# Queries times attention in a linear-attention kernel: from four products of 128 rows to eight of 64 rows at two row positions

## The reference

```
xn = layernorm(x);  q, k, v = xn @ Wq + bq, xn @ Wk + bk, xn @ Wv + bv
q = softmax(q, over the features of a head);  k = softmax(k, over the tokens)
attn[e, d] = sum over tokens s of k[s, e] * v[s, d]          # one small square per head
y[t, :]    = q[t, :] @ attn                                  # the "mix", per head
h = silu(layernorm(y) * (1 + scale) + shift) @ Wo + bo;  x = x + h
```

## Time and profile before

| | |
|---|---|
| median of 3 runs | 888.93 us (888.59 to 888.94) |
| the profiled execution | 892.45 us |
| its span in the trace | 890.7 us |
| TensorE busy (matmuls) | 847.7 us, 95% |
| VectorE, ScalarE, GpSimd busy | 683.3, 607.1, 550.8 us |
| mean granted clock of TensorE | 0.987 |

### The profile page before, as it was taken

How to read it: one execution, slowest core, us unless ns; L and a number is a source line. 1 busy time by engine, 2 the same in 40 slices (tenths; PEclk the granted TensorE clock), 3 DMA queues, 4 the chain that set the end, 5 groups by cost and what they waited for, 6 DMA issues and landing times.

```text
span 890.7 us, 19760 instructions
## 1 busy us (share of the span) xinstructions
PE 847.7 (95%) x6581; PEld 717.9 (81%) x6581; DVE 683.3 (77%) x1356; ACT 607.1 (68%) x1441; POOL 550.8 (62%) x741
## 2 busy tenths in 40 slices
PE   4988999899999999999987999999999999999997
PEld 4876878788787888888866878888888888888885
DVE  6976777687786787788876877877877788777665
ACT  6366676676666767777776767767766777776664
POOL 2566765666656657666756766676667666765641
PEclk9998999999999999999999999999999999999999
DMA  8686665666666555555664655566666556656431
GB/s 295 239 275 204 195 213 191 201 198 208 178 198 215 174 195 172 185 177 171 196 185 166 216 165 181 179 199 185 193 194 198 188 186 189 195 178 201 155 132 60
DMA packets 115482, 169.79 MB, mean 191 GB/s; under 512 B 11806, under 2 KB 84630, under 8 KB 115382
## 3 DMA queue, kind: packets, MB, share of 16 engines
q1 hardware_dynamic: 114880, 168.08, 59.4%
q10 hardware_dynamic: 502, 0.46, 0.2%
HBM read 95.61 MB, written 72.88 MB: 189 GB/s over the span
## 4 chain that ended last, share of the span: by engine, by line
PE 69%; DMA 11%; DVE 7%; ACT 4%; issue 4%; SPq 4%; POOL 1%; ACTq 0%; DVEq 0%; POOLq 0%
PE PS L943 60%; PE PS L1037 5%; DMA qy_turned<-QS 4%; PE PS L1021 3%; SPq L402 2%; DMA QT<-qy_turned 2%; DMA k_turned<-KT 1%; DMA x_turned<-XS 1%; SPq L417 1%; DMA STAGE<-in_wq 1%; DMA EK<-k_turned 1%; DMA XT<-x_turned 1%; ACT XF L786 1%; ACT SK L696 1%; SPq L377 1%
## 5 line engine op out<-in xcount | busy, mean ns | idle before, releaser
L592 POOL TENSOR_TENSOR HL<-H,HH 128x512 fp32r<-128x512 f32 x60 | 78.2, 1303 | 196.4 <-ACT HH L767 192.9
L734 ACT ACTIVATE Z<-QT,FC,FA 128x128 f32<-128x128 f32 x240 | 99.4, 486 | 114.4 <-DMA QT<-qy_turned 114.4
L943 PE MATMUL PS<-XH,WH_k 128*128 128x256 f32 x512 | 150.9, 295 | 3.9 <-DVE WL_k L319 3.9
L943 PE MATMUL PS<-XL,WH_k 128*128 128x256 f32 x512 | 145.7, 285 | 0.0
L943 PE MATMUL PS<-XH,WL_k 128*128 128x256 f32 x512 | 145.6, 284 | 0.0
L943 PE MATMUL PS<-WH_o,HH 128*128 128x512 f32 x248 | 106.8, 431 | 15.1 <-issue 14.8
L804 ACT ACTIVATE XN<-X,NBX,RSX 128x512 f32<-128x512 f32 x60 | 48.9, 815 | 82.4 <-POOL NBX L541 82.4
L943 PEld LDWEIGHTS PS<-XH,WH_k 128*128 128x128 f32 x512 | 99.0, 193 | 4.4 <-issue 4.2
L696 ACT ACTIVATE SK<-SK,KN 128x128 f32<-128x128 f32 x256 | 99.1, 390 | 3.5 <-DVE KN L1243 3.5
L943 PE MATMUL PS<-WH_q,XH 128*128 128x512 f32 x256 | 101.4, 396 | 0.0
L943 PE MATMUL PS<-WL_o,HH 128*128 128x512 f32 x248 | 101.0, 407 | 0.0
(11 more groups left out here) (155 smaller groups left out, 2121.5 us busy)
## 6 DMA issues: line engine op xcount, KB each, us to landing
qy_turned<-QS SPq DMA_DIRECT2D x60, 512.0 KB, 2.9
QT<-qy_turned SPq DMA_DIRECT2D x240, 128.0 KB, 3.0
k_turned<-KT SPq DMA_DIRECT2D x32, 512.0 KB, 4.1
EK<-k_turned SPq DMA_DIRECT2D x128, 128.0 KB, 2.8
x_turned<-XS SPq DMA_DIRECT2D x30, 512.0 KB, 2.9
XT<-x_turned SPq DMA_DIRECT2D x120, 128.0 KB, 3.4
out_x<-X SPq DMA_DIRECT2D x32, 256.0 KB, 3.4
X<-in_x SPq DMA_DIRECT2D x9, 512.0 KB, 5.3
```

The source lines that it names most:

```text
L592: eng.tensor_tensor(hl_of(o), h_of(o), hh_of(o).bitcast(F32), ALU.subtract).then_inc(pool_hl, 1)
L734: z = eng.activation(z_of(o)[:, c * P:c * P + P].rearrange("p (q n) -> p q n", q=Q), src, ACT.Identity, bias=FC[l][:, c, b:b + 1], scale=F ...
L943: mm = eng.matmul(dst, left[a](c), right[b](c), start=(c == 0 and a + b == 0), stop=(c == C - 1 and a == 1))
```

## The change

The contraction of the mix is cut in two. For each chunk c and each half u, 64 rows of EQ are the weights, at row position 0 or 64 of the array, and 66 columns stream through: for two heads of 32 (or one head of 64 as two pieces of 32), one column for the sum and 32 columns of the head. Half u writes to bank B_Y + u. That is eight products of 64x66 in place of four of 128x132. ATT shrinks from 128x528 to 128x264 elements, the attention products write into 256 columns of their bank instead of 512, the ScalarE copy reads 256 columns and writes them in runs of 32 with one column left free between them, and VectorE reads y in the new order (pieces of 33, the first the sum). The order of the work on every engine is as before; there are ten fewer rows of memsets on VectorE.

```
--- before.py
+++ after.py
-        ATT = sb("ATT", [P, 2, 2 * (P + Q)])
+        ATT = sb("ATT", [P, C, 2 * (32 + 1)])
...
-                eng.activation(ATT[:, :, Q:Q + 2 * P], PS[:, B_ATT, :].rearrange("p (b n) -> p b n", b=2), ACT.Copy)\
-                   .then_inc(act_att, 1)
+                eng.activation(ATT[:, :, :].rearrange("p c (h n) -> p (c h) n", h=2)[:, :, 1:],
+                               PS[:, B_ATT, 0:2 * P].rearrange("p (k n) -> p k n", n=32), ACT.Copy).then_inc(act_att, 1)
...
                 for c in range(C):
                     for f in range(0, P, 32):
                         a = f // w * w
+                        to = 64 * c + a % 64
                         vs = v[:, c * P + a:c * P + a + w]
                         ks = EK[:, f // 32, c // 2, t, c % 2, :]
-                        mm = eng.matmul(PS[f:f + 32, B_ATT, c * P + a:c * P + a + w],
+                        mm = eng.matmul(PS[f:f + 32, B_ATT, to:to + w],
                                         vs if l == 0 else ks, ks if l == 0 else vs,
                                         start=True, stop=True, tile_position=(0, f))
...
-                W = P + Q
+                W = 2 * (32 + 1)
                 for c in range(C):
-                    mm = eng.matmul(bank(B_Y + c // 2, (c % 2) * W, W), EQ[:, c * P:c * P + P],
-                                    ATT[:, c // 2, (c % 2) * W:(c % 2 + 1) * W], start=True, stop=True)
+                    for u in range(2):
+                        r = slice(64 * u, 64 * u + 64)
+                        mm = eng.matmul(bank(B_Y + u, c * W, W), EQ[r, c * P:c * P + P], ATT[r, c, :],
+                                        start=True, stop=True, tile_position=(64 * u, 0))
                 mm.then_inc(pe_y, 1)
...
-                ps = PS[:, B_Y:B_Y + 2, 0:Q]
-                sums = bass.AP(tensor=ps.tensor, offset=ps.offset, ap=[ps.ap[0], ps.ap[1], [Q + 2 * P, 2], [1, Q]])
-                then(eng.reciprocal(RQ[:, :].rearrange("p (b s q) -> p b s q", b=2, s=2), sums))
+                got = PS[:, B_Y:B_Y + 2, 0:2 * C * 33].rearrange("p u (k n) -> p u k n", n=33)
+                sums = RQ[:, :].rearrange("p (u k n) -> p u k n", u=2, n=1)
+                then(eng.reciprocal(sums, got[:, :, :, 0:1]))
...
-                eng.tensor_tensor(y.rearrange("p (b h n) -> p b h n", b=2, n=32),
-                                  PS[:, B_Y:B_Y + 2, Q:Q + 2 * P].rearrange("p b (h n) -> p b h n", n=32),
-                                  RQ[:, :].rearrange("p (b h) -> p b h", b=2).unsqueeze(3).to_broadcast([P, 2, 8, 32]),
+                five = [P, 2, C, 2, 32]
+                eng.tensor_tensor(y.rearrange("p (c u h n) -> p u c h n", c=C, u=2, h=2),
+                                  got[:, :, :, 1:33].rearrange("p u (c h) n -> p u c h n", h=2),
+                                  sums.rearrange("p u (c h) n -> p u c h n", h=2).to_broadcast(five),
                                   ALU.mult).then_inc(dve_yr, 1)
```

More of the change, by code:

```diff
@@ L1284, in second_ones @@
             def second_ones():
-                w = HEAD[1]
                 eng.wait_ge(pe_y, B)
[L1288 to L1291, removed]
+                for h in range(2):
+                    ins = eng.memset(ATT[:, :, 33 * h:33 * h + 1], 1.0)
                 ins.then_inc(dve_ones, 1)
@@ L1296, in zero_attention @@
                 eng.wait_ge(act_xf, 2 * FIRST)
-                eng.memset(PS[:, B_ATT, :], 0.0).then_inc(dve_zero, 1)
+                eng.memset(PS[:, B_ATT, 0:2 * P], 0.0).then_inc(dve_zero, 1)
             def mixed(j):
                 eng.wait_ge(pe_y, j + 1)
-                ps = PS[:, B_Y:B_Y + 2, 0:Q]
-                sums = bass.AP(tensor=ps.tensor, offset=ps.offset, ap=[ps.ap[0], ps.ap[1], [Q + 2 * P, 2], [1, Q]])
-                then(eng.reciprocal(RQ[:, :].rearrange("p (b s q) -> p b s q", b=2, s=2), sums))
+                got = PS[:, B_Y:B_Y + 2, 0:2 * C * 33].rearrange("p u (k n) -> p u k n", n=33)
+                sums = RQ[:, :].rearrange("p (u k n) -> p u k n", u=2, n=1)
+                then(eng.reciprocal(sums, got[:, :, :, 0:1]))
                 eng.wait_ge(dve_ys, min(j, LAST_Y))
@@ L1368, in start @@
                     a, z = 32 * g, 32 * g + 32
-                    eng.memset(ATT[a:z, :, g:g + 1], 1.0)
-                    eng.memset(ATT[a:z, :, 2 * P + Q + g:2 * P + Q + g + 1], 1.0)
+                    eng.memset(ATT[a:z, :, 33 * (g % 2):33 * (g % 2) + 1], 1.0)
                 eng.tensor_reduce(FOLD[:, :], ident[:, :].rearrange("p (g b) -> p b g", b=B), AX.X, ALU.add)
```

## The result

The kernel became slower: 900.74 us (897.34 to 905.36) against 888.93, ratio 1.0134, interval 1.0086 to 1.0181. The forecast was 904.4 us, with 880 to 916 as its range. The profiled execution took 905.36 us with a span of 903.6, so 12.9 us more than that of before. Times are medians, a ratio is worked out from the single executions and so is not exactly that of the medians. The ratios leave out executions over 1.5% above the fastest of their kernel, here two of the twelve of `eighths` (902.20 and 902.32 us).

A forecast was written before the change was run, and what follows sets the result against it. TensorE, busy 95% of the span, was taken to bound the kernel; 20.5 us for 64 longer mixes, less 0.2 for the copy and 4.8 for waits, gave +15.5 on 888.93: 904.4 us, range 880 to 916.

The forecast's parts named there:

- the sum: One mix, last output matmul to second keys matmul: 1.57 us against 1.25; 64 mixes give +20.5 us.
- the fold's rows: Conditioning fold: 128x128 float32 loads with 32 streamed columns also start 0.112 us apart, so the load sets the pace.
- Rival 2: Mix: the positions halve the work; -8 us (881), or -29 us (860) without entry and exit costs; chance 0.13.
- column positions: Attention: four column positions load side by side, 0.054 us for each four; two row positions assumed alike, eight pairs at 0.112.
- Rival 1: Mix: the two row positions load one after another, 16 at 0.112 us; +73 us, 962; chance 0.17.
- The turns: Going into and out of the divided array at each mix drains the engine; +0.32 us a mix.
- Entry: From the last output matmul to the mix's first matmul: 0.32 us, where an undivided one comes after 0.23.
- the load in the open: The mix's first weight load, no longer hidden: 0.10 us.
- exit: From the mix's last matmul to the recorded keys product: 0.15 us, where it was 0.04.
- the signs to look for: New trace: 1.5 to 1.6 us around a mix, first keys matmul 0.15 after it, 0.30 to the second.
- rival 3: Mix: nothing changes, since half rows need no change of array mode; 887 to 892 us; chance 0.10.
- What was given back: TensorE's waits in about 15 steps swallow 0.32 us each: 4.8 us, called an upper value.

The follow-up runs named there:

- eighths: Changed kernel with each product cut to weights of 64 rows by 32 columns, 32 products at eight positions: 895.31 us, ratio 1.006 to the kernel before.
- whole_66: Changed kernel with the mix back to four whole-array products of 128 rows, each streaming only 66 columns: 887.66 us, ratio 0.9974 to the kernel before.
- half_only: Changed kernel with only the four products at row position 0, half of y left out: 899.16 us, ratio 1.0112 to the kernel before.
- one_position: Changed kernel with all eight products of 64 rows at row position 0: 953.77 us, ratio 1.072 to the kernel before.
- whole_array: Changed kernel with the mix alone undone, four products of 128 rows by 132 columns on the whole array: 888.26 us, ratio 0.9976 to the kernel before.
- quads: Changed kernel with each product cut by tokens, 16 products of 64x64 weights at four positions: 882.98 us, ratio 0.9929; run again 886.22 us, 0.9961.
- quads_long_copy: Changed kernel with 64x64 weights at four positions and ScalarE's copy 512 columns wide again: 885.12 us, ratio 0.9957 to the kernel before.

## Why the prediction was right

**A whole load costs 0.112 us, however few columns stream.** Shown by whole_66: 66 or 132 columns, 1.25 us around the mix. That a stream of 132 columns takes as long as the load went unnoticed; it changes nothing in the sum, but the load is not alone in setting the pace before. The step from the fold's rows to the mix was the one that mattered most, for without it the halved columns look like a gain of 29 us.

**Fewer rows don't shorten a load.** 191 ns for 64 rows against 192 for 128, and half_only keeps the pace of 0.112. Rival 2 falls by this.

**Two row positions load side by side.** Shown twice: half_only is no faster, and one_position is 0.89 us slower around each mix. Rival 1 falls. This was a guess from column positions, and it held.

**The turns.** Entry 0.33 to the first matmul against a forecast of 0.32; the load in the open cost 0.05 and not 0.10; exit recorded at 0.20 against 0.15; the second keys matmul 0.22 later as in the sum (the signs to look for had said 0.30, in error). Together 1.59 against the 1.57 of the sum: two small misses cancel. half_only shows this price alone, and rival 3 falls. The Trainium skill's rule ("TensorEngine Tiling (Array Packing)", "Key Properties") that a change of mode drains the engine agrees with this trace, which adds the price: 0.33 us for a visit. The "up to 2x" of the Trainium skill ("TensorEngine Tiling (Array Packing)", "Theoretical Speedup") does not hold here: two positions only made up for the doubled number of loads.

**What was given back** is the term that was too small, and its reasoning was wrong. A step of layer 1 became 0.32 us longer, so 64 steps give the 20.5 us of the sum. The profiled executions differ by 12.9 and the medians by 11.8 and 12.6, so about 8 us came back, where the prediction had 4.8 and 0.2 for the copy.

The larger part is waits. The three kinds of the earlier trace rows fell from 25.7 to 21.0 us, and in the second profile of the changed kernel to 19.1. The prediction took 0.32 from each of 15 waits and called that an upper value; that 4.7 is close to its 4.8 is luck. What happened is that whole waits went. Here is the tenth attention in the kernel before, with the output products behind it:

```profile
170.84 0.46 PE L1021 MATMUL PS<-EK,VV 128*32 128x32 f32 x32
173.48 0.47 PE L943 MATMUL PS<-WH_o,HH 128*128 128x512 f32 x1 [2.18 <-issue]
...
174.49 0.62 PE L943 MATMUL PS<-WL_o,HH 128*128 128x512 f32 x1
174.91 0.63 PE L943 MATMUL PS<-WH_o,HL 128*128 128x512 f32 x1
```

And in the changed kernel:

```profile
177.12 0.46 PE L1022 MATMUL PS<-EK,VV 128*32 128x32 f32 x32
177.51 0.50 PE L943 MATMUL PS<-WH_o,HH 128*128 128x512 f32 x1
```

The 2.18 us are gone, not 0.32 of them. Not every wait shrank: the one behind the sixth attention (119.22 in the changed kernel) grew from 0.6 to 2.9 us. A likely reason is that the engines and transfers that feed TensorE gain on it in every longer step; no experiment singles that out. But the other profiles go the same way: with a mix of 1.25 us these waits are 25.7, 25.1 (whole_array) and 22.3 us (whole_66), with one of about 1.59 they are 21.0, 19.1 and 18.1 (half_only), and with one of 2.48 (one_position) 13.7. With the 1.17 of quads they are 18.9, but 6.8 us of waiting for GpSimd come on top. Which waits remain varies from execution to execution, and so does the time: the four timed executions of the changed kernel lie between 897 and 905 us.

The smaller part is the clock, which the prediction left out. Some waits are followed by a spell at the lower level of TensorE's clock (1.2 GHz), as the one above: from 174.50 to 177.90 the granted clock was 0.50, and the products there start 0.42 us apart instead of 0.23. Below are that stretch and the sum over all six such stretches between 48 and 520 us before; then one of the four after the change, and their sum:

```profile
174.50:177.90 3.40, 3.40 (x10) 2.63 (x8) 1.33 (x2) 1.44 (x3) 3.05 (x6) 0.50 0.78 210
...
sum 23.80, PE 21.42 PEld 17.39 DVE 11.44 ACT 14.59 POOL 19.26; mean PE 3.57 PEld 2.90 DVE 1.91 ACT 2.43 POOL 3.21
```

```profile
495.10:501.90 6.80, 6.13 (x35) 6.04 (x36) 5.56 (x11) 4.19 (x10) 5.42 (x9) 0.50 0.61 158
...
sum 20.60, PE 19.28 PEld 17.76 DVE 15.53 ACT 10.57 POOL 16.87; mean PE 4.82 PEld 4.44 DVE 3.88 ACT 2.64 POOL 4.22
```

At half the clock, 3.2 us less of it are worth at most 1.6 us. Waits and clock together are 6.3 of the 7.6 us that came back between the profiled executions; the rest was not located.

**Left open:** why whole_array is 0.24% faster than the kernel before. It is hardly the length of the copy (quads_long_copy), and not the mix, which takes 1.25 us there too. VectorE's order and the places in the banks were not tried apart, and the interval nearly reaches 1.

## What to carry to other kernels

Before a product is cut into smaller ones, find out whether its pace is set by the columns that stream or by those of the weights: look for another instruction in the same trace with the same weights and a different stream. Both can set it at once. Cutting the rows here halved the streamed columns and left the load as long as it was; cutting the weights' columns as well shortened both, and then four positions were worth it. Count the turn into and out of a divided array on each visit (0.33 us here), and put many products into one visit. On an engine that is nearly always busy, add the work up and then take off what waits will swallow; a wait of 2 us can go whole when each step grows by 0.32, so the longer step times the number of waits is no upper bound. A slow spell of the clock behind a wait can go with it.

## What was not expected of the hardware

- Four positions of 64x64 float32 weights run at 0.06 us for each four matmuls, but eight positions of 64x32 don't keep that pace: 64 matmuls took 0.64 us to start, the last ones about 17 ns apart.
- Loads of 128 float32 weight columns and streams of 132 float32 columns both allow a matmul each 0.11 us; with 66 columns a matmul can follow the one before it after 0.06, but the next load holds it (whole_66).
- The exit from the divided array is recorded at 0.20 us after a 64x128 mix and at 0.15 after one of 64x64, 609.92 - (609.29 + 0.70 - 0.22). On the whole array there is a like difference of 0.05: after a mix whose last matmul waits for its load and not for a stream (whole_66), the keys are recorded 0.08 us after that matmul, where it is 0.03 behind 132 columns.
- The kernel before is less steady than its first three runs (888.59 to 888.94) made it look: in later rounds its executions lay between 883.7 and 893.6 us. Differences of 0.2% need many rounds.
